# A Mamba block with a coupling layer on one core: ScalarE issues 29 of the transfers of each batch, x goes to another buffer, and two updates run by halves

## The chip, the cores and the metric

The program runs on one core of a Trainium2 chip. The metric is the device time of one execution in microseconds; the time of a kernel is the median of its runs. The engines are PE (TensorE), DVE (VectorE), ACT (ScalarE), POOL (GpSimd) and SP (SyncE, which computes nothing and only issues DMAs here). Every engine works through its own program in order; semaphores tie the programs together.

## The reference

Sixteen sequences of 1024 tokens with 256 channels go through two blocks, each with a residual and a layernorm.

```python
xi, res = split(x @ W_in.T + b_in)            # 512 channels each
xi = silu(causal depthwise conv(xi, 4 taps))
delta, B, C = split(xi @ W_x.T + b_x); delta = softplus(delta)   # 512, 16, 16
h = exp(delta * A) * h + delta * B * xi        # scan over tokens, 16 states per channel
y = (sum over states of h * C + xi * D) * silu(res)
x = layernorm(x + y @ W_out.T + b_out)
gf = global net of mean over tokens(x);  out = x
for _ in range(3):
    tf = sigmoid(small gelu net(out))          # one number per token
    out = out + (0.1 + range * 2 * (0.7 * gf + 0.3 * tf - 0.5)) * twist(out)
x = layernorm(x + out)
```

Twist swaps the two halves of the channels with signs. All is float32.

## The kernel before

**Units.** The scan of a batch is cut into 64 units: four blocks of 128 channels, each in four groups of 32 channels (a group on 128 partitions is 32 channels times 4 states), and four phases of 4 states for each group. There are 16 x 64 = 1024 units. For a unit ACT makes da = exp(delta_q * -A) in PSUM (L816), POOL makes dbx = u_q * b_quad in one of seven `work` buffers (L1060), DVE scans (L987), and the product with c_quad is made by DVE (L995) or, at the 26 positions of `POOL_AT`, by POOL three units later (L1067). PE sums the states into y_sum (L727), and every eight units DVE multiplies by the gates (L967).

**Side work.** All engines walk the same loop over t (one step per unit). At fixed positions within the period of 64 steps the tables `X_AT`, `RES_AT`, `DELTA_AT`, `O_AT` and so on place other work:
- for batch nb, one period ahead: x @ W_in, conv, silu (`SILU_AT` = 8, 32, 45, 55), gates ("r" tasks, into s_std), B and C rows ("c", into soft), delta for the next block ("d" tasks, ACT L938 to L944 into soft, DVE L1020 into delta, POOL L1082 makes u = delta * xi at DELTA_AT + 6 of each block);
- for batch f, one period behind: "o" (x + y @ W_out, L634 to L636, normalised by ACT into x1, which lies in the buffer `big`), "t" (transposed into oT), three cycles of the coupling net ("f", GELUs into big, tanh, DVE's products L1010 into big, POOL's updates of oT, L1075 and L1076), "g" (global net) and "e" (residual + oT + product, L665 to L668, normalised into oT, then stored to out).

PE's side work of step t is usually taken by DVE or ACT some steps later (`X_TAKE`, `O_RS` and so on). Three PSUM banks serve all of it, and a task waits until the one before has been read.

**Queues.** All DMAs are issued by SP, in the order of its program; where SP waits on a semaphore, everything behind it in its program waits too. SP's steps for step t are, in order: s_quad load, stores of delta and u, loads of delta_q and u_q (three copies of each; a group is loaded from DRAM after its store has landed and its slot is free), store of y, loads of yg, the x1 stores, the residual load (into the buffer yg), the out stores, the x_res load (L515, into oT, so it waits for the out stores), the gate stores (L405, four DMAs for each quarter), the x_feat load (L367), the bc stores (L536), and the loads of b_quad and c_quad. b_quad of phase 3 is loaded at position 63, behind three loads of c_quad, and is needed at the fourth unit of the next batch (unit 67 counted from this period's start).

**Around x_res.** x_res holds the batch's x for the residual of "o" and is read by PE at L636, after the four matmuls on yg; PE waits for both yg and x_res before the first matmul of "o". `first_gates` of batch 0 lie in s_std, big and oT.

Of the kernel before, what the change touches and what calls it, by code (L numbers as in the profile page):

```python
# [5 lines left out]
ALU = mybir.AluOpType  # L6
# [3 lines left out]
P = 128  # L10
BATCH, SEQ, DM = 16, 1024, 256
DI, NS, TAPS = 512, 16, 4
L = 512
DC = DI // P
# [72 lines left out]
RESST_AT = (4, 28, 47, 61)  # L87
X1ST_AT = (15, 16)
RES_IN_AT = 28
XRES_AT = 66  # L90
OUT_AT = (64, 64)
XFEAT_AT = 48
BCST_AT = 54
# [123 lines left out]
def build(nc, x, xT, weights, vectors, out):  # L217
# [7 lines left out]
    with ExitStack() as ctx:  # L225
# [65 lines left out]
        x_res = oT[:, :, :].rearrange("p m t -> p (m t)").rearrange("p (k c) -> p k c", c=DM)  # L291
# [73 lines left out]
        def _(sp):  # L365
# [37 lines left out]
            def store_gates(nb, n, gates, signal):  # L403
                for c in range(QUAD):
                    sp.dma_start(res_dram[nb % 2, n, c].rearrange("k p t -> p k t"),  # L405
                                 gates[GROUP * c:GROUP * c + GROUP, :].rearrange("p (k t) -> p k t", k=QUAD)) \
                      .then_inc(signal, 16)
# [63 lines left out]
            for t in range(FIRST, END):  # L471
# [20 lines left out]
                for h in range(2):  # L492
                    if (f := batch_at(t - PERIOD, X1ST_AT[h])) is not None:
                        sp.wait_ge(o_norm, 4 * f + 2 * h + 2)
                        sp.dma_start(x1_dram[f, h * L:(h + 1) * L, :].rearrange("(k p) c -> p k c", p=P),
                                     x1[:, 4 * h:4 * h + 4, :]).then_inc(x1_stored[h], 16)
                if (f := batch_at(t - PERIOD, RES_IN_AT)) is not None:
                    for h in range(2):
                        sp.wait_ge(x1_stored[h], 16 * (f + 1))
                    sp.wait_ge(o_ready, 4 * f + 4)  # L500
                    sp.dma_start(residual, x1_dram[f].rearrange("(k p) c -> p k c", p=P)).then_inc(re_in, 16)
                for h in range(2):
                    if (f := batch_at(t - PERIOD, OUT_AT[h])) is not None:
                        sp.wait_ge(e_norm, 4 * f + 2 * h + 2)
                        for r in range(2):
                            sp.dma_start(out[f, h * L:(h + 1) * L, :].rearrange("(n r p) c -> r p n c", p=P, r=2)[r],
                                         oT[:, r, h * L:(h + 1) * L].rearrange("p (n c) -> p n c", n=2)) \
                              .then_inc(out_done[h], 16)
                if (f := batch_at(t, XRES_AT)) is not None:
                    if f == 0:  # L510
                        sp.wait_ge(first_stored[DC - 1], 64)
                    if f:
                        for h in range(2):
                            sp.wait_ge(out_done[h], 32 * f)
                    sp.dma_start(x_res, x[f].rearrange("(k p) c -> p k c", p=P)).then_inc(xr_in, 16)  # L515

                for n in range(DC):
                    if ahead == RESST_FIRST[n]:
                        sp.wait_ge(r_taken, 2 * n + 2)
                        store_gates(0, n, first_gates[n], first_stored[n])  # L520
                    if (nb := batch_at(ahead, RESST_AT[n])) is not None and nb:
                        sp.wait_ge(res_ready, DC * (nb - 1) + n + 1)
                        store_gates(nb, n, s_std, res_stored)
                nb = 0 if ahead == XFEAT_FIRST else batch_at(ahead, XFEAT_AT)
                if nb is not None and nb + 1 < BATCH and (nb or ahead == XFEAT_FIRST):
                    sp.wait_ge(r_ready, 8 * nb + 8)
                    load_x_feat(nb + 1)
                nb = 0 if ahead == BCST_FIRST else batch_at(ahead, BCST_AT)
                if nb is not None and (nb or ahead == BCST_FIRST):
                    for j in range(PHASE):  # L530
                        if nb:
                            sp.wait_ge(c_in_[j], 16 * nb)
                            sp.wait_ge(b_in_[j], 16 * nb)
                    sp.wait_ge(c_taken, nb + 1)
                    for k in range(QUAD):
                        sp.dma_start(bc_dram[:, QT * k:QT * k + QT], first_or(nb, first_rows, bc_rows)[GROUP * k:GROUP * k + GROUP, :]) \  # L536
                          .then_inc(bc_stored, 16)
# [20 lines left out]
        def _(pe):  # L558
# [65 lines left out]
            def couple(kind, f, n, bank):  # L624
                shared = banks[:, bank, :]
                if kind == "o":
                    pe.wait_ge(yg_in[n % 2], 64 * (2 * f + n // 2 + 1))
                    if n == 0:
                        pe.wait_ge(xr_in, 16 * (f + 1))
                    for r in range(2):  # L630
                        tb = 2 * n + r
                        half = shared[:, r * DM:(r + 1) * DM]
                        for k in range(4):
                            pe.matmul(half, yg[:, n % 2, k, r * P:r * P + P], w_out[:, k, :], start=k == 0, stop=False)  # L634
                        pe.matmul(half, eye, b_out, start=False, stop=False)
                        mm = pe.matmul(half, eye, x_res[:, tb, :], start=False, stop=True)  # L636
# [503 lines left out]
```

## Time and profile before

| | us |
|---|---|
| median of 3 runs | 4038.7 |
| lowest, highest | 4038.14, 4043.2 |
| the profiled execution | 4040.28 |
| its span, first to last instruction | 4038.5 |
| mean granted TensorE clock | 0.946 of full speed |

| engine | busy us | share |
|---|---|---|
| POOL | 3644.6 | 90% |
| PE | 3524.4 | 87% |
| DVE | 3429.6 | 85% |
| ACT | 2959.0 | 73% |

The span has a start of 60 us (weights, the first conv), sixteen periods of some 240 us, and an end of about 140 us in which the last batch's coupling runs alone. An idle time in brackets stands before the instruction of its row, with what ended it.

### The profile page before, as it was taken

How to read it: one execution, taken by the hardware profiler on the slowest of the kernel's cores; microseconds unless marked ns; L12 is line 12 of the kernel's file. 1: busy time of each engine (PE TensorE's matmuls, PEld its weight loads, DVE VectorE, ACT ScalarE, POOL GpSimd, SP SyncE). 2: the span in 40 equal slices, each digit the busy share in tenths (PEclk: the TensorE clock that was granted, in tenths of full speed). 3: DMA queues.
4: the chain of work that ended last, by engine and by line, in shares of the span. 5: the costliest groups of instructions: out<-in, count | busy, mean ns of one | idle time of the engine just before them, and what ended most of it. 6: DMA issues, size and time to landing. Idle time of an engine off the chain costs nothing. (4 is left out here: it accounts for less than half of the span.)

```text
span 4038.5 us, 51729 instructions
## 1 busy us (share of the span) xinstructions
PE 3524.4 (87%) x18776; PEld 1611.5 (40%) x18776; DVE 3429.6 (85%) x2508; ACT 2959.0 (73%) x3918; POOL 3644.6 (90%) x1604
## 2 busy tenths in 40 slices
PE   7669989899998998989898998989989898897766
PEld 3224353443434344353443434344353443434233
DVE  4988988889898898989889898898989889898861
ACT  4447868778786877868777786877868777785753
POOL 4999999999999999999999999999999999999860
PEclk9779999999999999999999999999999999998888
DMA  5354373543536354373644546454363544546320
GB/s 182 130 175 154 128 230 120 188 152 130 186 130 224 129 191 138 122 229 120 197 148 155 159 152 200 140 187 129 133 218 123 194 149 158 160 138 199 127 86 31
DMA packets 329645, 630.04 MB, mean 156 GB/s; under 512 B 27952, under 2 KB 226608, under 8 KB 329136
## 3 DMA queue, kind: packets, MB, share of 16 engines
q1 hardware_dynamic: 329392, 626.74, 47.0%
q8 instruction: 150, 2.46, 0.3%
q14 instruction: 103, 0.84, 0.1%
HBM read 456.76 MB, written 169.87 MB: 155 GB/s over the span
## 5 line engine op out<-in xcount | busy, mean ns | idle before, releaser
L1060 POOL TENSOR_TENSOR work<-u_q,b_quad 128x1024 f32<-128x1024 f32 x1024 | 2397.3, 2372 | 138.2 <-DMA u_q<-u_scratch 97.1
L816 ACT ACTIVATE da<-delta_q,neg_a 128x1024 f32<-128x1024 f32 x1024 | 1126.3, 1112 | 600.9 <-DVE work L995 430.8
L987 DVE TENSOR_TENSOR_SCAN da<-da,work 128x1024 f32<-128x1024 f32 x608 | 1389.9, 2286 | 151.4 <-ACT da L816 119.7
L1067 POOL TENSOR_TENSOR work<-work,c_quad 128x1024 f32<-128x1024 f32 x416 | 985.2, 2368 | 11.6 <-DVE work L987 11.3
L987 DVE TENSOR_TENSOR_SCAN work<-da,work 128x1024 f32<-128x1024 f32 x416 | 945.9, 2278 | 29.9 <-ACT da L816 28.1
L727 PE MATMUL y_sum<-work,v_all 128*32 128x256 f32 x8192 | 613.3, 399 | 303.3 <-POOL work L1067 190.7
L995 DVE TENSOR_TENSOR work<-da,c_quad 128x1024 f32<-128x1024 f32 x608 | 743.9, 1224 | 28.6 <-DMA c_quad<-bc_scratch 4.6
L752 ACT ACT_TABLE_LOAD x563 | 722.3, 1283 | 14.5 <-DMA v_all<-in_vectors 3.9
L727 PEld LDWEIGHTS y_sum<-work,v_all 128*32 128x32 f32 x8192 | 199.8, 110 | 771.0 <-issue 259.3
L613 PE MATMUL banks<-xi,w_all 128*128 128x512 f32 x1024 | 479.8, 612 | 9.4 <-ACT g_act L797 5.1
L600 PE MATMUL banks<-xi,taps 128*128 128x512 f32 x984 | 453.2, 606 | 0.0
L681 PE MATMUL banks<-oT,w_all 128*128 128x512 f32 x768 | 389.7, 635 | 16.8 <-POOL oT L1076 16.7
L606 PE MATMUL banks<-x_feat,w_all 128*128 128x512 f32 x512 | 278.6, 684 | 27.5 <-DVE big L1010 26.7
L613 PEld LDWEIGHTS banks<-xi,w_all 128*128 128x128 f32 x1024 | 188.2, 192 | 259.4 <-issue 237.4
L634 PE MATMUL banks<-w_all,yg 128*128 128x256 f32 x1024 | 262.6, 402 | 30.8 <-DMA oT<-in_x 30.8
L591 PE MATMUL banks<-x_feat,w_all 128*128 128x512 f32 x512 | 256.0, 636 | 26.5 <-ACT big L787 17.2
L600 PEld LDWEIGHTS banks<-xi,taps 128*128 128x128 f32 x984 | 179.4, 191 | 244.1 <-issue 244.1
L787 ACT ACTIVATE big<-banks,v_all 128x512 f32<-128x512 f32 x336 | 218.9, 685 | 66.8 <-PE banks L681 47.0
L1082 POOL TENSOR_TENSOR soft<-delta,xi 128x1024 f32<-128x1024 f32 x64 | 151.2, 2362 | 112.1 <-DVE delta L1020 112.1
L634 PEld LDWEIGHTS banks<-w_all,yg 128*128 128x128 f32 x1024 | 200.9, 200 | 85.6 <-issue 58.5
L681 PEld LDWEIGHTS banks<-oT,w_all 128*128 128x128 f32 x768 | 136.0, 196 | 197.5 <-issue 183.3
L1010 DVE TENSOR_TENSOR big<-banks,oT 128x1024 f32<-128x1024 f32 x96 | 112.6, 1214 | 93.5 <-PE banks L703 93.5
(86 smaller groups left out, 3270.3 us busy)
## 6 DMA issues: line engine op xcount, KB each, us to landing
delta_q<-delta_scratch SPq DMA_DIRECT2D x256, 512.0 KB, 5.8
u_q<-u_scratch SPq DMA_DIRECT2D x256, 512.0 KB, 6.1
delta_scratch<-delta SPq DMA_DIRECT2D x64, 512.0 KB, 2.9
u_scratch<-soft SPq DMA_DIRECT2D x64, 512.0 KB, 2.9
b_quad<-bc_scratch SPq DMA_DIRECT2D x64, 512.0 KB, 4.7
c_quad<-bc_scratch SPq DMA_DIRECT2D x64, 512.0 KB, 7.1
s_quad<-res_scratch SPq DMA_DIRECT2D x128, 256.0 KB, 4.1
y_scratch<-s_quad SPq DMA_DIRECT2D x128, 256.0 KB, 3.2
```

What stands on the lines that cost most here:

```text
L600: mm = pe.matmul(banks[:, bank, to:], taps[:, m, k, :], xi[:, nb % 2, m, half * L + to - s:half * L + L - s], start=k == 3, stop=k == 0)
L606: mm = pe.matmul(banks[:, bank, :], w_in[:, k, DI + m * P:DI + m * P + P], x_feat[:, k, half * L:half * L + L], start=k == 0, stop=k == 1)
L613: mm = pe.matmul(banks[:, bank, :], w_x[:, k, m * P:m * P + P], xi[:, nb % 2, k, half * L:half * L + L], start=k == 0, stop=k == 3)
L634: pe.matmul(half, yg[:, n % 2, k, r * P:r * P + P], w_out[:, k, :], start=k == 0, stop=False)
L681: mm = pe.matmul(shared, w1[:, k, m * P:m * P + P], oT[:, k, half * L:half * L + L], start=k == 0, stop=k == 1)
L727: mm = pe.matmul(y_sum[GROUP * i:GROUP * i + GROUP, cols], fold, work[:, un % WORK, QT * i:QT * i + QT], start=False, stop=done)
L752: nc.scalar.preload_act_table_set(name)
L816: act.activation(da[:, t % 2, :], delta_q[:, slot, :], ACT.Exp, scale=neg_a[:, t % PERIOD:t % PERIOD + 1]).then_inc(da_ready, 1)
L987: dve.tensor_tensor_scan(dst, da[:, t % 2, :], work[:, slot, :], 0.0, ALU.mult, ALU.add) \
L995: dve.tensor_tensor(work[:, slot, :], da[:, t % 2, :], c_quad[:, j, :], ALU.mult).then_inc(prod_dve, 1)
L1060: pool.tensor_tensor(work[:, slot, :], u_q[:, copied, :], b_quad[:, j, :], ALU.mult) \
L1067: pool.tensor_tensor(work[:, un % WORK, :], work[:, un % WORK, :], c_quad[:, un % PHASE, :], ALU.mult) \
```

## The change

ACT issues the DMAs of what it makes: the x1 stores, the out stores, the gate stores of batches 1 and later, their bc stores, and also the x_feat load (from batch 2 on), the residual load and the x_res load. They stand in ACT's program some steps after the instruction that makes the data, with the same waits; the first batch's gate and bc stores stay with SP. x_res lies in `big` (the x1 buffer) and not in oT; it is loaded at position 63 instead of 66 and waits for the batch before's "e" products on PE (`e_ready`) instead of the out stores. The wait for the out stores moves to ACT's first "t" take. In "o" PE multiplies x_res and b_out first and waits for yg only then; in "e" it waits for the last coupling product only after three matmuls. POOL's two updates are made half by half, and PE's first matmuls of the next cycle wait for their own half.

```diff
-XRES_AT = 66
+XRES_AT = 63
-        x_res = oT[:, :, :].rearrange("p m t -> p (m t)").rearrange("p (k c) -> p k c", c=DM)
+        x_res = x1
@@ PE, "o"
-                    pe.wait_ge(yg_in[n % 2], 64 * (2 * f + n // 2 + 1))
                     if n == 0:
                         pe.wait_ge(xr_in, 16 * (f + 1))
                     for r in range(2):
...
+                        pe.matmul(half, eye, x_res[:, tb, :], start=True, stop=False)
+                        pe.matmul(half, eye, b_out, start=False, stop=False)
+                        if r == 0:
+                            pe.wait_ge(yg_in[n % 2], 64 * (2 * f + n // 2 + 1))
                         for k in range(4):
-                            pe.matmul(half, yg[:, n % 2, k, r * P:r * P + P], w_out[:, k, :], start=k == 0, stop=False)
-                        pe.matmul(half, eye, b_out, start=False, stop=False)
-                        mm = pe.matmul(half, eye, x_res[:, tb, :], start=False, stop=True)
+                            mm = pe.matmul(half, yg[:, n % 2, k, r * P:r * P + P], w_out[:, k, :],
+                                           start=False, stop=k == 3)
@@ PE, first matmuls of a cycle
-                            pe.wait_ge(updated, (CYCLES - 1) * f + c)
+                            pe.wait_ge(updated, 2 * ((CYCLES - 1) * f + c - 1) + half + 1)
@@ ACT, in its loop over t
+                    for h in range(2):
+                        if pos == O_AT[2 * h + 1] + O_RS + 1:
+                            act.wait_ge(o_norm, 4 * f + 2 * h + 2)
+                            act.dma_start(x1_dram[...], x1[:, 4 * h:4 * h + 4, :]).then_inc(x1_stored[h], 16)
+                        if pos == E_AT[2 * h + 1] + O_RS + 1:
+                            act.wait_ge(e_norm, 4 * f + 2 * h + 2)
+                            for r in range(2):
+                                act.dma_start(out[...], oT[...]).then_inc(out_done[h], 16)
+                    if pos == RES_IN_AT:
...
+                        act.dma_start(residual, x1_dram[f].rearrange("(k p) c -> p k c", p=P)).then_inc(re_in, 16)
...
+                if (f := batch_at(t, XRES_AT)) is not None:
+                    if f == 0:
+                        act.wait_ge(first_stored[1], 64)
+                        act.wait_ge(first_stored[2], 64)
+                    else:
+                        act.wait_ge(e_ready, 4 * f)
+                    act.dma_start(x_res, x[f].rearrange("(k p) c -> p k c", p=P)).then_inc(xr_in, 16)
...
+                        if pos == SILU_AT[m] + 1:
+                            act.wait_ge(res_ready, DC * (nb - 1) + m + 1)
+                            for c in range(QUAD):
+                                act.dma_start(res_dram[...], s_std[...]).then_inc(res_stored, 16)
+                    if pos == RES_AT[7] + RES_TAKE + 1 and nb + 1 < BATCH:
+                        act.wait_ge(r_ready, 8 * nb + 8)
+                        act.dma_start(x_feat[:, :, :], xT[nb + 1].rearrange("(k p) t -> p k t", p=P)).then_inc(xf_in, 16)
+                    if pos == BC_AT + BC_TAKE + 1:
...
+                        for k in range(QUAD):
+                            act.dma_start(bc_dram[:, QT * k:QT * k + QT], bc_rows[...]).then_inc(bc_stored, 16)
@@ POOL
-                            pool.wait_ge(f_prod, 2 * cycle + 2)
-                            pool.tensor_tensor(oT[:, 0, :], oT[:, 0, :], big[:, 1, :], ALU.add)
-                            pool.tensor_tensor(oT[:, 1, :], oT[:, 1, :], big[:, 0, :], ALU.subtract).then_inc(updated, 1)
+                            for half in range(2):
+                                cols = slice(half * L, half * L + L)
+                                pool.wait_ge(f_prod, 2 * cycle + half + 1)
+                                pool.tensor_tensor(oT[:, 0, cols], oT[:, 0, cols], big[:, 1, cols], ALU.add)
+                                pool.tensor_tensor(oT[:, 1, cols], oT[:, 1, cols], big[:, 0, cols], ALU.subtract) \
+                                    .then_inc(updated, 1)
```

## Rows read from the trace of the kernel before

**Rows 1.** The page, busy time, share of the span and instructions of each engine

```profile
PE 3524.4 (87%) x18776; PEld 1611.5 (40%) x18776; DVE 3429.6 (85%) x2508; ACT 2959.0 (73%) x3918; POOL 3644.6 (90%) x1604
```

**Rows 2.** Waits of POOL, 60 to 3900 us: us in total, times, longest

```profile
POOL work L1060 <- DMA u_q<-u_scratch: 97.1, 44, 4.0
POOL soft L1082 <- DVE delta L1020: 77.9, 20, 7.0
POOL work L1060 <- DMA b_quad<-bc_scratch: 37.0, 17, 10.4
```

**Rows 3.** Waits of SP's queue, whole span

```profile
SPq L405 <- ACT s_std L918: 366.1, 31, 16.2
...
SPq L367 <- PE banks L606: 145.7, 15, 10.3
```

**Rows 4.** Waits of all engines, whole span: DVE's scan

```profile
DVE da L987 <- ACT da L816: 119.7, 135, 16.1
...
DVE da L987 <- POOL work L1060: 29.9, 35, 3.0
```

**Rows 5.** Timeline of POOL, one period: start, duration, row, idle before

```profile
1864.68 2.36 POOL L1060 TENSOR_TENSOR work<-u_q,b_quad 128x1024 f32<-128x1024 f32 x1 [0.51 <-DMA u_q<-u_scratch]
...
1920.94 2.35 POOL L1067 TENSOR_TENSOR work<-work,c_quad 128x1024 f32<-128x1024 f32 x1 [0.46 <-DVE work L987]
...
1935.36 7.01 POOL L1060 TENSOR_TENSOR work<-u_q,b_quad 128x1024 f32<-128x1024 f32 x3 [2.77 <-DMA u_q<-u_scratch]
...
1956.22 2.39 POOL L1082 TENSOR_TENSOR soft<-delta,xi 128x1024 f32<-128x1024 f32 x1
...
1969.57 2.34 POOL L1060 TENSOR_TENSOR work<-u_q,b_quad 128x1024 f32<-128x1024 f32 x1 [1.72 <-DMA u_q<-u_scratch]
...
1980.50 4.67 POOL L1060 TENSOR_TENSOR work<-u_q,b_quad 128x1024 f32<-128x1024 f32 x2 [1.64 <-DMA b_quad<-bc_scratch]
```

**Rows 6.** Timeline of SP's queue, the same period

```profile
1857.18 1.79 SPq L405 DMA_DIRECT2D res_scratch<-s_std  x4
...
1928.27 0.39 SPq L367 DMA_DIRECT2D x_feat<-in_xT  x1
...
1929.27 0.53 SPq L400 DMA_DIRECT2D u_q<-u_scratch  x1
```

**Rows 7.** Timeline of PE, the same period

```profile
1944.74 0.64 PE L727 MATMUL y_sum<-work,v_all 128*32 128x256 f32 x8 [1.39 <-POOL work L1067]
...
1971.41 0.39 PE L668 MATMUL banks<-v_all,big 128*128 128x128 f32 x2
```

**Rows 8.** Timeline of DVE, the same period

```profile
1907.73 2.30 DVE L987 TENSOR_TENSOR_SCAN da<-da,work 128x1024 f32<-128x1024 f32 x1 [1.50 <-ACT da L816]
...
1955.39 0.75 DVE L1020 SCALAR_TENSOR_TENSOR delta<-banks,v_all,soft 128x512 f32<-128x512 f32 x1 [0.30 <-ACT soft L944]
```

**Rows 9.** Timeline of ACT: the exp of unit 64 of this period

```profile
1968.25 1.12 ACT L816 ACTIVATE da<-delta_q,neg_a 128x1024 f32<-128x1024 f32 x1 [3.19 <-DMA delta_q<-delta_scratch]
```

**Rows 10.** Busy time in 1972 to 1976 us; last: clock, DMA share, GB/s

```profile
1972.00:1976.00 4.00, 1.86 (x32) 0.64 (x24) 3.69 (x3) 1.12 (x1) 4.00 (x2) 1.00 0.92 353
```

**Rows 11.** Groups of instructions: busy us, mean ns of one, idle before

```profile
L1010 DVE TENSOR_TENSOR big<-banks,oT 128x1024 f32<-128x1024 f32 x96 | 112.6, 1214 | 93.5 <-PE banks L703 93.5
...
L1075 POOL TENSOR_TENSOR oT<-oT,big 128x1024 f32<-128x1024 f32 x32 | 75.2, 2351 | 90.6 <-DVE big L1010 90.6
...
L1037 POOL TENSOR_TENSOR coef<-v_all 128x1 f32<-128x1 f32 x1 | 0.2, 193 | 0.1
```

**Rows 12.** Timeline of PE, the end of the run

```profile
3920.20 3.75 PE L634 MATMUL banks<-w_all,yg 128*128 128x256 f32 x8 [14.76 <-DMA oT<-in_x]
...
3975.46 9.67 PE L681 MATMUL banks<-oT,w_all 128*128 128x512 f32 x16 [7.00 <-POOL oT L1076]
...
4020.82 0.67 PE L665 MATMUL banks<-yg,v_all 128*128 128x256 f32 x2 [1.28 <-DVE big L1010]
```

**Rows 13.** Timeline of SP's queue, the end of the run

```profile
3910.39 1.94 SPq L441 DMA_DIRECT2D yg<-y_scratch  x4
```

**Rows 14.** The page, DMA issues: count, KB each, median us to landing

```profile
yg<-y_scratch SPq DMA_DIRECT2D x256, 128.0 KB, 3.7
```

More of the change, by code:

```diff
@@ L401, in load_u, with store_first_gates @@
                              .broadcast_to([GROUP, QUAD, SEQ])).then_inc(uq_in[slot], 16)
[L403 removed]
+            def store_first_gates(n):
                 for c in range(QUAD):
[L405 to L407 removed]
+                    sp.dma_start(res_dram[0, n, c].rearrange("k p t -> p k t"),
+                                 first_gates[n][GROUP * c:GROUP * c + GROUP, :].rearrange("p (k t) -> p k t", k=QUAD)) \
+                      .then_inc(first_stored[n], 16)
             def load_s_quad(pair):
@@ L491, in _ @@
                         load_yg(f, n)
[L492 to L515, printed above, removed]
                 for n in range(DC):
@@ L519, in _ @@
                         sp.wait_ge(r_taken, 2 * n + 2)
[L520 to L534, printed above, removed]
+                        store_first_gates(n)
+                if ahead == XFEAT_FIRST and BATCH > 1:
+                    sp.wait_ge(r_ready, 8)
+                    load_x_feat(1)
+                if ahead == BCST_FIRST:
+                    sp.wait_ge(c_taken, 1)
                     for k in range(QUAD):
-                        sp.dma_start(bc_dram[:, QT * k:QT * k + QT], first_or(nb, first_rows, bc_rows)[GROUP * k:GROUP * k + GROUP, :]) \
+                        sp.dma_start(bc_dram[:, QT * k:QT * k + QT], first_rows[GROUP * k:GROUP * k + GROUP, :]) \
                           .then_inc(bc_stored, 16)
@@ L659, in couple @@
                     pe.wait_ge(re_in, 16 * (f + 1))
-                    pe.wait_ge(f_prod, 2 * (CYCLES * f + CYCLES - 1) + n // 2 + 1)
                     for r in range(2):
@@ L667, in couple @@
                             pe.matmul(half[:, m * P:m * P + P], oT[:, m, tokens], eye, start=False, stop=False)
+                        if r == 0:
+                            pe.wait_ge(f_prod, 2 * (CYCLES * f + CYCLES - 1) + n // 2 + 1)
+                        for m in range(2):
                             mm = pe.matmul(half[:, m * P:m * P + P], big[:, 1 - m, tokens], minus if m else eye,
@@ L819, in _ @@
                 for f, pos in couplings(t):
+                    for h in range(2):
+                        if pos == O_AT[2 * h + 1] + O_RS + 1:
+                            act.wait_ge(o_norm, 4 * f + 2 * h + 2)
+                            act.dma_start(x1_dram[f, h * L:(h + 1) * L, :].rearrange("(k p) c -> p k c", p=P),
+                                          x1[:, 4 * h:4 * h + 4, :]).then_inc(x1_stored[h], 16)
+                        if pos == E_AT[2 * h + 1] + O_RS + 1:
+                            act.wait_ge(e_norm, 4 * f + 2 * h + 2)
+                            for r in range(2):
+                                act.dma_start(out[f, h * L:(h + 1) * L, :].rearrange("(n r p) c -> r p n c", p=P, r=2)[r],
+                                              oT[:, r, h * L:(h + 1) * L].rearrange("p (n c) -> p n c", n=2)) \
+                                   .then_inc(out_done[h], 16)
+                    if pos == RES_IN_AT:
+                        for h in range(2):
+                            act.wait_ge(x1_stored[h], 16 * (f + 1))
+                        act.wait_ge(o_ready, 4 * f + 4)
+                        act.dma_start(residual, x1_dram[f].rearrange("(k p) c -> p k c", p=P)).then_inc(re_in, 16)
                     for n in range(4):
@@ L826, in _ @@
                             act.wait_ge(t_ready, 4 * f + n + 1)
+                            if n == 0 and f:
+                                for h in range(2):
+                                    act.wait_ge(out_done[h], 32 * f)
                             act.activation(oT[:, m, half * L:half * L + L], banks[:, BANK_OF["t", f, n], :],
```

16 lines of the change are left out of this document (11 added, 5 removed).

## Prediction

> **What bounds the kernel now.** I read the busy shares first, then who POOL waits for, then SP's own waits, then one period of 240 us (one batch, 64 units) engine by engine, then the end of the run. POOL is busy 90%, DVE 85%, PE 87%, ACT 73% [rows 1]. That makes POOL look like the bound, with idle time in three groups: 97 us until u_q lands, 78 us until delta is made, 37 us until b_quad lands [rows 2]. The u_q waits are SP's doing: SP is an in-order queue that stood 366 us before the gate stores and 146 us before the x_feat loads, with u_q loads queued behind [rows 3]. In the period that I read, the u_q stall of 2.77 us before unit 56 [rows 5] comes from a load issued at 1929.27, just behind the x_feat load at 1928.27 [rows 6], and the one at unit 36 from loads behind the four gate stores at 1857.18 [rows 6].
>
> The question is whether those stalls are on the path. Over the run DVE's scans waited 119.7 us for ACT's da and only 29.9 us for POOL's products [rows 4]. So POOL is not ahead of a chain that hangs on it: in the second half of a period ACT and DVE set the pace. Three rows say so. DVE's scan at 1907.73 waits 1.50 us for ACT [rows 8]; POOL at 1920.94 waits 0.46 us for DVE [rows 5]; and POOL's u at 1956.22 starts 0.08 us after delta's second half is done (1955.39 + 0.75) [rows 5, 8]. POOL's lost time in this half is mostly slack that it must give back at the next of these meetings.
>
> **Part 1: loads no longer stand behind SP's waits.** The unit-36 stall (0.51 us here; the 44 u_q waits of the run average 2.2 us [rows 2]) ends before POOL next meets DVE (a product with a wait of 0.46 at 1920.94), so I count 0 for it; if all of it were on the path, 2 us per batch. The unit-56 stall of 2.77 us is different. It delays POOL's product of unit 55, for which PE waited 1.39 us just before the next block's delta matmuls [rows 7], and those lead to ACT's soft, DVE's delta and POOL's u. Without the stall the next thing late is PE's own work, after ACT's silu. So the worth is 1.39 of the 2.77 us: -1.39 us x 14 batches = -19 us. Bounds: 0 and -2.8 x 14 = -39 us.
>
> **Part 2: 29 DMA issues per batch move to ACT.** 16 gate stores, 4 bc stores, 4 out stores, 2 x1 stores, residual, x_res and x_feat. Four gate stores took SP 1.79 us [rows 6], 0.45 each; the trace of before has no DMA issued by ACT, so this is the nearest row. Total 29 x 0.45 = 13 us per batch, on an engine with 27% idle. Most falls where ACT is waiting anyway, so it costs nothing there. Where ACT runs dense and DVE waits for its da, it counts: the gate stores after silu at positions 33 and 46 (the scan that waited 1.50 us for ACT at 1907.73 is at 46, [rows 8]). Each burst is queued behind an exp of 1.1 us (1.12 in [rows 9]). If the queue issues while that exp runs, 1.8 - 1.1 = 0.7 us is left; otherwise 1.8; and 0 if ACT issues faster than SP. I take 0.6 each, 1.2 per batch, against the 1.39 won in part 1 on the same chain: net -0.2 us x 14 = -3 us. Bounds: -1.39 and +2.2 us per batch (-19 to +31 us). The waits ahead of these DMAs are on ACT's own results or on transfers long done, with one exception.
>
> **Part 3: x_res.** ACT now waits at position 63 for all four "e" products. PE finishes the fourth at 1971.8 [rows 7]. ACT's next exp (unit 64) started at 1968.25 [rows 9] and would start at about 1972.2, 4 us late; what is queued behind is that exp, the third normalise and the first two out stores. DVE's scan of unit 64 slips about 0.6 us, which the b_quad stall three units later swallows. I count 0; bound +0.6 x 15 = +9 us.
>
> But the load itself moves. It used to go out after the out stores; now 1 MB of x, and 0.5 MB of out, start at about 1972, when the DMA engines already moved 353 GB/s at a busy share of 0.92 [rows 10] and the last b_quad load is still to come. POOL waited 1.64 us for that b_quad at 1980.50 [rows 5], in the part of the period in which POOL does set the pace. 1.5 MB at 353 GB/s is 4.2 us if all of it went ahead; the gate stores of 0.5 MB that stood there move away, worth 1.5 us; and two queues share instead of queueing. Between -0.5 and +3 us per batch; I take +0.8: +0.8 x 15 = +12 us. The Trainium skill (DMA: Bandwidth & Descriptors, Queues, rings and completion order) says that an SDMA engine goes round the queue rows packet by packet. By it SP's b_quad is slowed by x_res and not put behind it; no row of before shows two issuing queues.
>
> The longest u_q stall is 4.0 us [rows 2], not 2.77; for the few at unit 56 that are longer than in my period I count another -3 us in all.
>
> **Part 4: updates by halves.** POOL runs 64 ops of 2.35 us [rows 11] as 128. With 193 ns for a one-column op [rows 11], half an op is 0.193 + 511 x 2.11 ns = 1.27 us, so a pair costs 0.2 us more: 0.8 us per batch. It falls where POOL waits for DVE at the next meeting (0.46 us at 1920.94) and has just been freed of the unit-36 stall: 0. Without this cover, +12 us.
>
> **Part 5: the end of the run.** After the last scan nothing hides. PE waited 14.76 us for x_res until 3920.20 [rows 12]; now only yg is waited for. Its four issues began at 3910.39 and took 1.94 us [rows 13], landing takes 3.7 us [rows 14]: 3916.0, and up to 1 us less, because the out stores no longer stand ahead. With two of the matmuls done before, PE has saved about 5.5 us. Each of the two updates: PE waited 7.00 us until 3975.46 [rows 12]. Behind the first half of DVE's product there used to be the second half (1.21 us) and two whole updates (4.70 us) [rows 11]; now it is one pair of halves, 2.54 us: 1.21 + 4.70 - 2.54 = 3.4 us earlier, twice, 6.7 us. The second half is ready before PE asks. "e" starts three matmuls before the product: 0.9 of the 1.28 us of wait at 4020.82 [rows 12]. Together -13 us, bounds -9 and -17.
>
> **Sum.** -13 - 3 - 3 + 12 = -7, plus about -1 for x_res's own wait gone within periods: -8 us. The profiled execution took 4040.3 us (span 4038.5), 1.6 above the median of 4038.7: 4032 by the profile, 4030.5 by the median. Predicted: 4030.
>
> **Rivals.**
> 1. Slower, x_res in front of b_quad. Place: POOL at unit 67. For: DMA near saturation there [rows 10]; each us lost is POOL's and DVE's together. Against: the queues share, and the gate stores leave. At 3 us per batch: 4038.7 - 13 - 6 + 45 = 4065. It makes the kernel slower from about 1.4 us per batch (21 us against 13 + 6). Chance 0.17.
> 2. ACT becomes the bound: issues aren't hidden under the exp, 1.8 us per burst: 4038.7 - 13 + 31 = 4057 with contention at 0. For: ACT is dense and DVE waits for it [rows 4]. Against: 27% idle overall. Chance 0.12.
> 3. The SP stalls are worth more: ACT's issues are hidden and contention is nil: 4038.7 - 13 - 19 - 5 = 4002. If POOL's time counts in full (2 + 2.8 us per batch), 4038.7 - 13 - 70 = 3956. For: POOL's 90%. Against: POOL has to meet DVE between. Chance 0.24 for near 4002, 0.05 for near 3956.
> 4. The issuer does not matter: only the order and the end change, 4038.7 - 13 = 4026. The Trainium skill (DMA: Bandwidth & Descriptors, Issuing engines are not separate DMA queues) says that issuing from several engines saves only the time that the sequencer takes to issue. By it parts 1 and 2 are nearly nothing; but the rows show that SP's queue loses its time in waits, 366 us at one line [rows 3], which the rule does not speak of. Chance 0.07.
>
> The forecast itself (4012 to 4045) has 0.35. A measurement of this kernel can tell about 0.2%, 8 us. Below 4030.6: rivals 3 and 4 and not quite half of the forecast, 0.50; within 8 us either way 0.24; above 4046.8 rivals 1 and 2 less a little, 0.26. The range for 8 in 10 reaches from inside rival 3 to inside rival 1: 3985 to 4068.
>
> **What would show it.** Right: SP's waits at the gate stores and x_feat gone, POOL's u_q idle down from 97 us to about 40 (the wait at unit 64 stays), but POOL's waits for delta and for DVE's products up by nearly as much. ACT's DMA issues visible at about 0.45 us. POOL's b_quad waits up from 37 us to about 50. In the tail PE starts "o" near 3915 instead of 3920 and the two 7 us waits become 3.7. Wrong: a period well below 239 us, with POOL's waits for DVE not grown, means that the SP stalls were on the path; b_quad waits of 70 us or more mean rival 1; DVE's wait for da far above 120 us means rival 2.

## The result and the profile after

| | before | after |
|---|---|---|
| median us (8 runs each) | 4038.09 | 4060.28 |
| lowest, highest | 4033.76, 4046.72 | 4051.1, 4067.87 |
| ratio of the times, 95% interval | | 1.0046 [1.0035, 1.0058] |
| span of the profiled execution | 4038.5 | 4058.3 |

The change makes the kernel 0.46% slower, about 20 us. The forecast was 4030 us, 8 us faster than before. Of the executions that the later sections compare, two (5821 us and 4160 us, at a granted clock of 0.55 and 0.87) ran in a slower state of the chip and are left out.

The first thing to read is where along the run the 20 us lie. The table is worked out from the starts of DVE's 1024 scans, as means over the periods 1 to 14, in us.

| stretch | before | after | difference |
|---|---|---|---|
| units 0 to 8 of a period | 27.0 | 28.8 | +1.8 |
| 8 to 15 | 30.0 | 30.8 | +0.8 |
| 15 to 28 | 51.9 | 51.5 | -0.4 |
| 28 to 36 | 28.1 | 27.5 | -0.6 |
| 36 to 46 | 38.8 | 38.7 | -0.1 |
| 46 to 56 | 36.0 | 36.0 | 0 |
| 56 to 64 | 29.5 | 29.6 | +0.1 |
| period, from scan 64 to scan 960, by 14 | 241.23 | 242.86 | +1.63 |
| first period; last period | 227.3; 233.0 | 228.4; 235.8 | +1.1; +2.8 |
| last scan to the end | 135.1 | 128.6 | -6.5 |

14 x 1.63 = 22.8, with 1.1 and 2.8 that is 26.7, less 6.5 is 20.2; the first scan comes 0.5 earlier. The loss is in units 0 to 15 of each period, right behind the place where x_res is loaded (position 63 of the period before); the units behind them win back 1.0 us.

The waits of POOL from 60 us on, beside [rows 2] (us in total, times, longest):

```profile
POOL soft L1096 <- DVE delta L1031: 76.7, 33, 7.0
POOL work L1071 <- DMA b_quad<-bc_scratch: 76.6, 17, 11.4
POOL work L1071 <- DMA u_q<-u_scratch: 46.4, 27, 3.8
POOL work L1078 <- DVE work L998: 42.6, 60, 3.5
```

The u_q waits are halved (97.1 to 46.4), and POOL now waits for DVE's products instead (L1078, 42.6 us; before it was 11.3 us). So 31 of the 51 us are slack which changed its name. The b_quad waits doubled, 37.0 to 76.6 us, and one of the 17 is the one at the start of the run. DVE shows whose time that is. Its scan's waits from 300 to 3900 us, first before, then after:

```profile
DVE da L987 <- ACT da L816: 99.9, 132, 3.3
DVE da L987 <- POOL work L1060: 20.4, 28, 1.4
```

```profile
DVE da L998 <- ACT da L781: 110.1, 145, 3.6
DVE da L998 <- POOL work L1071: 38.1, 27, 2.6
```

The wait for POOL's products grew from 20.4 to 38.1 us, since POOL's stalls reach DVE; the wait for ACT grew by 10 only.

SP's waits changed their name too. Its 366.1 us at the gate stores [rows 3] are gone, but an in-order queue then stands at the next thing that isn't ready, here the store of y. That wait, before and after, over the whole span:

```profile
SPq L428 <- DVE s_quad L967: 500.5, 54, 23.4
```

```profile
SPq L423 <- DVE s_quad L978: 848.6, 69, 23.4
```

One such stall, read engine by engine. ACT's queue (ACTq is ACT's DMA issue) around position 63, in the trace of after:

```profile
1990.31 0.40 ACTq L862 DMA_DIRECT2D big<-in_x  x1
1990.81 1.12 ACT L781 ACTIVATE da<-delta_q,neg_a 128x1024 f32<-128x1024 f32 x1 [7.56 <-PE banks L633]
1990.83 1.23 ACTq L793 DMA_DIRECT2D out<-oT  x2
```

SP's queue and POOL at the same time:

```profile
1986.41 6.89 SPq L441 DMA_DIRECT2D c_quad<-bc_scratch  x3
1993.39 0.69 SPq L441 DMA_DIRECT2D b_quad<-bc_scratch  x1
...
1992.67 4.69 POOL L1071 TENSOR_TENSOR work<-u_q,b_quad 128x1024 f32<-128x1024 f32 x2
2001.79 4.66 POOL L1071 TENSOR_TENSOR work<-u_q,b_quad 128x1024 f32<-128x1024 f32 x2 [4.43 <-DMA b_quad<-bc_scratch]
```

The 1 MB of x_res leave at 1990.31, 0.5 MB of out at 1990.83, and the last b_quad load at 1993.39. POOL can go on at 2001.79, 8.4 us after the issue; before it was 1974.91 to 1980.50, 5.6 us. (The medians over batches 2 to 15 are 8.6 and 5.5 us.) The stall is 4.43 us where it was 1.64 [rows 5]. What the DMA engines moved behind the issue (the last numbers of a row: clock, DMA share, GB/s), before and after:

```profile
1974.00:1978.00 4.00, 2.41 (x33) 0.87 (x34) 3.65 (x6) 0.78 (x2) 4.00 (x3) 1.00 0.80 323
1978.00:1981.00 3.00, 3.00 (x8) 1.32 (x9) 3.00 (x4) 2.90 (x9) 1.36 (x2) 1.00 0.56 224
```

```profile
1994.00:1998.00 4.00, 2.62 (x20) 1.01 (x21) 3.97 (x8) 3.24 (x8) 3.36 (x2) 1.00 1.01 336
1998.00:2002.00 4.00, 4.00 (x11) 1.85 (x10) 3.90 (x3) 3.48 (x6) 0.21 (x1) 1.00 1.03 409
```

Before, the engines had room while b_quad was on its way (a share of 0.80, then 0.56). After, they are full until it has landed.

### The profile page after: what moved, and what is told of

Same layout as the page of the kernel before. It is cut to its first block and busy times, and to the rows that moved or that the text cites. A ratio compares the mean times of both kernels' runs of the same rounds, so it can differ in the third digit from the quotient of the medians.

```text
span 4058.3 us, 51746 instructions
## 1 busy us (share of the span) xinstructions
PE 3531.5 (87%) x18776; PEld 1621.1 (40%) x18776; DVE 3429.1 (84%) x2508; ACT 2960.5 (73%) x3918; POOL 3655.3 (90%) x1668
## 5 line engine op out<-in xcount | busy, mean ns | idle before, releaser
L1071 POOL TENSOR_TENSOR work<-u_q,b_quad 128x1024 f32<-128x1024 f32 x1024 | 2394.9, 2367 | 127.3 <-DMA b_quad<-bc_scratch 76.6
L1078 POOL TENSOR_TENSOR work<-work,c_quad 128x1024 f32<-128x1024 f32 x416 | 983.0, 2363 | 42.6 <-DVE work L998 42.6
L574 PE MATMUL banks<-xi,w_all 128*128 128x512 f32 x1024 | 493.1, 626 | 9.5 <-ACT g_act L762 5.1
L598 PE MATMUL banks<-w_all,yg 128*128 128x256 f32 x1024 | 245.3, 383 | 4.5 <-DMA yg<-y_scratch 4.5
```

Source lines behind the costliest of these rows:

```text
L574: mm = pe.matmul(banks[:, bank, :], w_x[:, k, m * P:m * P + P], xi[:, nb % 2, k, half * L:half * L + L], start=k == 0, stop=k == 3)
L598: mm = pe.matmul(half, yg[:, n % 2, k, r * P:r * P + P], w_out[:, k, :], start=False, stop=k == 3)
L1071: pool.tensor_tensor(work[:, slot, :], u_q[:, copied, :], b_quad[:, j, :], ALU.mult) \
L1078: pool.tensor_tensor(work[:, un % WORK, :], work[:, un % WORK, :], c_quad[:, un % PHASE, :], ALU.mult) \
```

## The experiments

All ratios are to the kernel before, run beside the changed one each time, with a 95% interval; its median lay between 4038 and 4046 us, so ratios are to be compared and not times. "Period" and "tail" (last scan to the end) are those of the table above. The theory at the outset: rival 1's mechanism, x_res and out in front of b_quad. Its rivals: a wait that ACT took over, and the cost of ACT's issues.

**x_res for one batch only.** It leaves out 15 of the 16 x_res loads; the wait for the "e" products stays.

```diff
+                    if f == 0:
                         act.dma_start(x_res, x[f].rearrange("(k p) c -> p k c", p=P)).then_inc(xr_in, 16)
@@ PE, "o"
-                        pe.wait_ge(xr_in, 16 * (f + 1))
+                        pe.wait_ge(xr_in, 16)
```

> The changed kernel, but x is loaded into the x1 buffer for batch 0 only; the 15 later loads of 1 MB are left out (later batches add a stale buffer), while ACT still waits for the e products at the same place. My theory (x_res competes with the last b_quad load, +2 us per batch, and with the last store of y in the tail): POOL's b_quad waits fall from 76.6 us to 40 or less, the b_quad load lands in about 5.6 us after its issue and not 8.3, and the time falls by 25 to 35 us, to about 0.994 to 0.998 of the kernel before. Rival (ACT standing up to 8.6 us before e_ready delays the exp of unit 64 and with it everything): time stays within 5 us of the changed kernel, 1.004 to 1.006, whatever the b_quad wait does. Second rival (the out stores are what collides): b_quad waits stay above 60 us.

Measured: 0.9925 [0.9904, 0.9946]. The b_quad waits are 36.2 us, the period 240.07, units 0 to 8 take 26.3 us. The wait on ACT is still there and harmless:

```profile
ACT da L781 <- PE banks L633: 100.5, 14, 8.1
```

So it is the load's bytes, and not the wait that stands ahead of it. (The next run, which has no such wait though it has the bytes, has a period only 0.3 us shorter.) The gain over the changed kernel, 1.2% or 49 us, is more than the 25 to 35 us that I expected.

**x_res by SP, behind the last b_quad and c_quad loads.** All is kept, and only the place differs.

```diff
-    (ACT) act.wait_ge(e_ready, 4 * f) ; act.dma_start(x_res, ...)
+    (SP, after load_b and load_c of the step) sp.wait_ge(e_ready, 4 * f) ; sp.dma_start(x_res, ...)
```

> The changed kernel, but SP issues the x_res load, in its own order behind the last loads of b_quad and c_quad (same wait for the e products). Theory of contention: b_quad goes first in one queue, b_quad waits fall to about 45 us (the out stores still share), ACT's wait for e_ready is gone; time 15 to 25 us below the changed kernel, 0.998 to 1.001 of before. If only the ACT wait mattered: the same gain here but none in the run without the loads. If neither: 1.0046 as the changed kernel.

Measured: 0.9901 [0.9883, 0.9919], 4007.27 us: faster than before by 1%, and well below the 0.998 to 1.001 that I expected. The period is 239.74, 3.1 us less than after, and units 0 to 8 take 26.5 us. SP's queue and POOL:

```profile
1967.37 0.65 SPq L441 DMA_DIRECT2D b_quad<-bc_scratch  x1
1968.11 0.55 SPq L441 DMA_DIRECT2D c_quad<-bc_scratch  x1
1968.71 0.58 SPq L514 DMA_DIRECT2D big<-in_x  x1
...
1972.23 4.67 POOL L1071 TENSOR_TENSOR work<-u_q,b_quad 128x1024 f32<-128x1024 f32 x2 [0.91 <-DMA b_quad<-bc_scratch]
```

With x_res issued 1.3 us behind it instead of 3.1 us ahead of it, b_quad is there 4.9 us after its issue instead of 8.4; the median is 5.5 us, as before the change. One more thing moves in this run: ACT no longer stands at the "e" wait, so the first out half goes out 6.7 us ahead of b_quad instead of 2.8.

**Is it the issuer or the place?** Two runs cross the two: x_res stays on ACT but goes out three units later, and x_res goes to SP but ahead of the last b_quad load.

```diff
-XRES_AT = 63
+XRES_AT = 66
```

> The changed kernel with the x_res load still issued by ACT but at position 66 instead of 63, so some 4 to 6 us after the last b_quad load is issued. Theory (what collides is the time at which 1 MB starts, not ACT as issuer): b_quad waits 45 to 60 us (the first out half still collides), ACT's wait for e_ready is gone, time 15 to 35 us below the changed kernel, 0.996 to 1.001 of before; PE may wait a little for x_res before o. Rival (it has to be SP's queue, in order behind b_quad): within 8 us of the changed kernel.

```diff
+    (SP, ahead of load_b and load_c of the step) sp.wait_ge(e_ready, 4 * f) ; sp.dma_start(x_res, ...)
```

> The run with x_res by SP, but in SP's order the x_res load stands just ahead of the last b_quad load and not behind the last c_quad. One queue, 1 MB in front: at 353 GB/s that is 2.8 us more until b_quad lands. Theory (bandwidth ahead of b_quad is the whole harm): b_quad waits 34 + 15 x 2 to 3 = 65 to 80 us, the time about that of the changed kernel less its out part, 1.000 to 1.005 of before. Rival (two queues sharing is worse than one in order): b_quad waits under 50 us and a ratio under 0.995.

Measured: 0.9938 [0.9922, 0.9955] on ACT at 66, with b_quad waits of 42.9 us; and 1.0047 [1.0029, 1.0065] by SP ahead of b_quad, with 80.1 us, the same as after. One queue, SP's, in the run that is slow:

```profile
1986.39 0.86 SPq L505 DMA_DIRECT2D big<-in_x  x1
1987.34 0.54 SPq L441 DMA_DIRECT2D b_quad<-bc_scratch  x1
...
1995.31 4.66 POOL L1071 TENSOR_TENSOR work<-u_q,b_quad 128x1024 f32<-128x1024 f32 x2 [4.92 <-DMA b_quad<-bc_scratch]
```

From b_quad's issue to POOL's start are 8.0 us, against 8.4 with two queues (medians 7.8 and 8.6; in this run b_quad also goes out 0.7 us later for POOL, since SP first waits for "e" and issues x_res). The issuer is not the cause of the loss; the megabyte started ahead of b_quad is. Between ACT at 66 and SP behind the quads 0.4% remain. By the profiled executions (spans 4016.8 and 4005.4 us) nearly all of it lies in the periods, 0.76 us each; the tail is only 1.0 us longer, though the late x_res makes PE wait 10.6 us for it there. Why ACT at 66 is the worse place was not tested.

**The out stores.** Both halves at position 67, x_res still on ACT at 63.

```diff
-                        if pos == E_AT[2 * h + 1] + O_RS + 1:
+                        if pos == E_AT[3] + O_RS + 1:
```

> The changed kernel; both halves of the out stores are issued by ACT at position 67, behind the last normalise, instead of the first half at position 64. x_res stays on ACT at 63. Theory (x_res's 1 MB does most of the harm, the first 0.5 MB of out a part): b_quad waits fall from 76.6 to 55 to 70 us, time 3 to 12 us below the changed kernel (1.002 to 1.004 of before). Rival (the out stores collide, x_res not): b_quad waits near 37 us and 0.993 of before.

Measured: 0.9988 [0.9976, 0.9999]; b_quad waits 54.3 us, period 241.58. The first out half, a third of the bytes ahead of b_quad, is worth 0.58%, or 23 us, where I expected 3 to 12: 1.3 us of each period, and 4 us at the end of the run (most of these at another granted clock, see Part 5 below).

The runs together show what b_quad's way costs. The table is worked out from the traces, medians over batches 2 to 15 in us; a start with a minus lies ahead of b_quad's issue, one with a plus behind it.

| run | x_res starts | first out half starts | b_quad's issue to POOL's start |
|---|---|---|---|
| before | +11.5, SP | +1.9, SP | 5.5 |
| after | -3.4, ACT | -2.8, ACT | 8.6 |
| x_res for one batch only | not loaded | -3.0, ACT | 5.5 |
| out late | -3.1, ACT | +5.7, ACT | 6.7 |
| x_res by SP ahead of b_quad | -0.7, SP | -7.3, ACT | 7.8 |
| x_res by SP behind | +1.3, SP | -6.7, ACT | 5.5 |
| x_res by ACT at 66 | +4.6, ACT | -6.7, ACT | 6.0 |
| x_res and bc by SP, out late (below) | +1.3, SP | +5.5, ACT | 5.0 |

Against the 5.0 us with nothing of the two ahead, half a megabyte of out alone costs 0.5 us, x_res alone on ACT 1.7, both together 3.6: what these transfers cost doesn't add up. x_res right ahead in b_quad's own queue costs 2.3 us (7.8 against 5.5).

**Part 1: what the two stalls on SP were worth.** One puts the x_feat load back on SP at its old place, the other the gate stores.

```diff
-    (ACT) act.wait_ge(r_ready, 8 * nb + 8) ; act.dma_start(x_feat, ...)
+    (SP, position 48) sp.wait_ge(r_ready, 8 * nb + 8) ; load_x_feat(nb + 1)
```

> The changed kernel, but SP issues the x_feat load at its old place. Theory: the u_q stall of 2.8 us before unit 56 comes back (u_q waits from 46 up to about 85 us). By the prediction it cost 1.39 us per batch on PE ahead of the delta matmuls; but the changed kernel gives that back in ACT's wait for bc_scratch, so I expect 0 to 8 us slower than the changed kernel (1.0046 to 1.0065 of before). Rival (not on the path at all): within 2 us. Rival (fully on the path): 20 to 39 us slower, 1.009 to 1.014.

```diff
-    (ACT, SILU_AT[m] + 1) act.wait_ge(res_ready, ...) ; four act.dma_start(res_dram, ...)
+    (SP, positions 4, 28, 47, 61) sp.wait_ge(res_ready, ...) ; four sp.dma_start(res_dram, ...)
```

> The changed kernel, but SP issues the gate stores again at its old positions. Theory: SP's waits there only made POOL stall where it has slack against DVE and ACT, so the u_q waits rise from 46 us by about 25 us (the stall at unit 36 comes back), POOL's waits for delta and for DVE's products fall by about as much, and the time stays within 5 us of the changed kernel; the scans from unit 36 to 46 and 46 to 56 stay at 38.6 and 36.0 us. Rival (the SP stalls at the gate stores were on the path): 15 us or more slower than the changed kernel. Rival (ACT pays for these issues): faster by 10 us or more.

Measured: x_feat on SP 1.0090 [1.0072, 1.0109], period 244.18 (my expectation was too low; this is my rival "fully on the path", at its lower edge); gates on SP 1.0035 [1.0024, 1.0046], period 242.85. POOL's waits, first with x_feat on SP, then with the gates on SP:

```profile
POOL work L1072 <- DMA u_q<-u_scratch: 82.0, 37, 4.4
POOL work L1079 <- DVE work L999: 20.8, 31, 3.4
```

```profile
POOL work L1071 <- DMA u_q<-u_scratch: 73.1, 41, 3.8
POOL work L1078 <- DVE work L998: 25.2, 25, 3.8
```

Both bring back u_q waits, 35.6 and 26.7 us. In the first the program loses 0.44%, 18 us (1.32 us per period, 0.8 of them in units 56 to 64, behind the stall that comes back); in the second it loses nothing. POOL's sums don't tell the two apart: its waits for DVE's products shrink by 21.8 us in the first and by 17.4 in the second. Where the stall stands does.

**Part 2: ACT's wait for the bc stores.** The ACT timeline of after shows a wait that my working had not:

```profile
1960.15 1.28 ACT L717 ACT_TABLE_LOAD   x1
1960.16 1.28 ACTq L870 DMA_DIRECT2D res_scratch<-s_std  x3
...
1964.98 1.12 ACT L781 ACTIVATE da<-delta_q,neg_a 128x1024 f32<-128x1024 f32 x1 [0.99 <-DVE work L998]
1965.30 1.74 ACTq L882 DMA_DIRECT2D bc_scratch<-soft  x4
1968.29 0.69 ACT L949 ACTIVATE soft<-banks,soft_bias 128x512 f32<-128x512 f32 x1 [2.19 <-DMA bc_scratch<-soft]
```

The bc stores now stand behind an exp that waits for DVE, so they go out late, and ACT's next write to soft waits until they have landed: 35.5 us in 15 waits, before 3.8 in 2. This kernel gives the bc stores back to SP at position 54.

> The changed kernel, but SP issues the bc stores of batches 1 and later again, at its old place. Theory: in the changed kernel the store is queued on ACT behind the exp of position 58, so ACT's next soft waits for its landing (35.5 us in 15 waits) and the 1.4 us won on PE before the delta matmuls are lost. With SP: that wait is gone or under 5 us, delta of the last block is made about 1 to 1.4 us earlier per batch, time 12 to 20 us below the changed kernel (1.000 to 1.002 of before). Rival: the delta chain isn't what the next batch waits for (it waits for u_q and b_quad transfers), then the time falls by less than 5 us though the wait is gone.

Measured: 1.0028 [1.0014, 1.0042]; ACT's wait falls from 35.5 to 17.3 us, the period by 0.3 us. Beside after's 1.0046 that is some 7 us, and the intervals overlap: a small loss, likely but not certain, and less than the 12 to 20 us that I expected. Half of ACT's wait is still there.

**Part 4 and 5: updates whole again.**

```diff
-                            for half in range(2): ... oT[:, 0, cols] ... oT[:, 1, cols] ... .then_inc(updated, 1)
+                            pool.wait_ge(f_prod, 2 * cycle + 2)
+                            pool.tensor_tensor(oT[:, 0, :], ...); pool.tensor_tensor(oT[:, 1, :], ...).then_inc(updated, 2)
```

> The changed kernel with POOL's two updates whole again (64 ops of 2.35 us instead of 128 of 1.27), PE's next cycle still waiting for both. Theory: inside the periods the halves cost and bring nothing; in the tail they save 3.3 us twice. So this run is 5 to 8 us slower than the changed kernel (1.0058 to 1.0066 of before), and PE's two waits of 3.8 us in the tail are 7 us again. Rival (128 ops cost POOL, the busiest engine, 0.8 us per batch on the path): this run is 5 us or more faster than the changed kernel.

Measured: 1.0060 [1.0043, 1.0076]. The period is 242.79 (after 242.86), so the halves cost nothing within it; the tail is 133.7 us, 5.1 more than after. PE's two waits in the tail are 14.2 us with whole updates; in after they are:

```profile
3997.86 9.64 PE L646 MATMUL banks<-oT,w_all 128*128 128x512 f32 x16 [3.75 <-POOL oT L1089]
...
4020.71 10.15 PE L646 MATMUL banks<-oT,w_all 128*128 128x512 f32 x16 [3.84 <-POOL oT L1089]
```

**SP issues everything.** Does the issuer matter at all? Every transfer is on SP at its old place, x_res late as in the second run, with the new order in "o" and "e" and the halves.

> The changed kernel with every DMA issued by SP, at the old places in SP's order, except x_res, which SP issues behind the last loads of b_quad and c_quad (into the x1 buffer, as in the run with x_res by SP). What is left of the change: the other buffer and place for x_res, the order of the matmuls in o and e, the updates by halves. Theory (the issuer is worth nothing in the periods, the ACT and DVE chain sets the pace from unit 28 on; the gain of the run with x_res by SP came from x_res and the end of the run): 0.990 to 0.995 of before, within 0.2% of the run with x_res by SP. Rival (freeing SP's queue is what makes that run fast, once the x_res collision is gone): 0.996 to 1.001, near before less the 6 to 10 us of the tail.

Measured: 0.9950 [0.9935, 0.9965], period 240.62, tail 121.6; u_q waits are back at 91.0 us, and SP stands again where it stood:

```profile
SPq L512 <- ACT s_std L930: 361.6, 31, 16.0
```

Against 0.9901 with ACT issuing, ACT's issuing is worth about 0.5%, 20 us, where my theory said less than 0.2%. That is about what the x_feat place was worth by itself (18 us above); no run splits it here. The other half of the gain over before needs no second queue.

**The mended versions.** First x_res and bc by SP and both out halves late; then also the last b_quad load a unit earlier, ahead of the second c_quad load.

> The run with x_res by SP (ratio 0.9901), with the bc stores on SP and the out stores of both halves at position 67 as well. Theory (each removes a cause found: bc landing before soft, sharing with b_quad): b_quad waits near 34 us or below, ACT's wait for bc landing under 20 us, ratio 0.985 to 0.990. Rival (the last block's delta isn't what the next batch waits for): within 0.1% of 0.990.

```diff
-LB_AT, LC_AT = (59, 55, 57, 63), (61, 62, 61, 63)
+LB_AT, LC_AT = (59, 55, 57, 62), (61, 63, 61, 63)
```

> Starts from the mended version (x_res, the bc stores and x_res behind the quads on SP, both out halves late) and changes only the order of two loads: the last b_quad load of a batch goes out at unit 62, ahead of the second c_quad load, instead of behind it. In the mended version POOL still waits 29.5 us in all for b_quad: one wait of 10.9 us at the start of the program and about 1.2 us per batch. Theory: that per-batch wait is the last thing that holds POOL, and through POOL the DVE, in the stretch around units 4 to 8. Then the b_quad waits fall to about 12 us in all, the period falls by 1.0 to 1.6 us, and the time against the kernel before is 0.984 to 0.988 of it. Rival: the wait is taken over by the next one, either c_quad (now later) or a DVE result that POOL needs; then the b_quad waits fall but another POOL or DVE wait grows by as much, and the time stays at 0.989 to 0.992.

Measured: 0.9904 [0.9887, 0.9921], no better than x_res alone moved, as the rival said: b_quad waits 29.5 us and ACT's wait for bc 17.5 us are as my theory had them, the time is not. So with x_res out of the way, neither the late out stores nor the bc stores on SP are worth more than the 10 us or so that the intervals leave. Then 0.9869 [0.9852, 0.9885], 3994.76 us, the fastest of all. In the last one POOL waits for b_quad only at the start of the run. POOL's two lines, first without, then with the earlier load:

```profile
POOL work L1078 <- DVE work L998: 46.1, 59, 3.4
...
POOL work L1071 <- DMA b_quad<-bc_scratch: 29.5, 17, 10.9
```

```profile
POOL work L1078 <- DVE work L998: 52.4, 63, 3.4
...
POOL work L1071 <- DMA b_quad<-bc_scratch: 11.9, 2, 10.5
```

Of the 17.6 us some went to waits for DVE (+6.3) and for u_q (+4.6). Units 8 to 15 take 1.1 us less, and units 15 to 46 take 0.8 us more. The times put it in the theory's range. The two profiled executions don't: both spans are 3995.8 us, and the periods are 239.27 and 239.03. They were the fastest execution of the one kernel and the slowest of the other, and the two intervals all but touch. That the order of these two loads is worth something is likely; how much, between 0 and 14 us, stays open.

## Why the prediction was wrong, step by step

The measured 4060 us lie within the stated 3985 to 4068, but the kernel became slower where the forecast was faster. Of the signs named in advance, "b_quad waits of 70 us or more mean rival 1" came: 76.6 us.

- **What bounds the kernel, and the unit-36 stall at 0: right.** The gates on SP bring 27 us of u_q waits back and cost nothing.
- **Part 1, -19 us for x_feat: right.** 18 us measured (the two intervals leave 6 to 30), 1.32 us per period against 1.39 in the working. The closeness of the two is in part luck: 0.5 of the 1.32 us lie outside units 56 to 64.
- **Part 2, issues on ACT at 1.2 us per batch (+17 us within the net of -3): wrong, it is 0.** An issue takes about what was expected (1.28 us for three, 1.74 for four, though 1.23 for the two of out), but the three at 1960.16 run beside ACT's table load. "Each burst is queued behind an exp" asked the right question, and of its three answers 0 was the right one. The bursts stand at positions 33 and 46 and the x_feat load at 51; the stretches 28 to 36, 36 to 46 and 46 to 56 take 27.5, 38.7 and 36.0 us, before 28.1, 38.8 and 36.0. Rival 2 falls with it.
- **Part 2, "the waits ahead of these DMAs are on ACT's own results or on transfers long done": true, and beside the point.** What delays a DMA on a computing engine is also the instruction before it, here an exp that waited for DVE. I had asked what queues behind the DMA's wait, but not what the DMA queues behind and who waits until it has landed. Some 7 us by one run, within the noise by another.
- **Part 3, x_res at +0.8 us per batch (+12 us): this term lost the case.** By the run with x_res moved behind b_quad it is 3.1 us per period, some 45 us, and 53 us (4058.3 less 4005.4) with the first and last periods and the end; some 3 of the 4.6 us at the end are a lower granted clock (Part 5). Rival 1 had the mechanism, its price (3 us per batch) and its total (4065, measured 4060), with a chance of 0.17. That its total fits is in part luck: it took 13 us for the end where 6.5 came, and 6 us for parts 1 and 2 where more came. Where the working went wrong: "1.5 MB at 353 GB/s is 4.2 us if all of it went ahead" was the right bound. I then took away 1.5 us for gate stores that leave, and discounted for two queues that share. But the way of b_quad grew by 3.1 us per batch all the same, so sharing and the gate stores together gave back about a quarter of 4.2 us, not four fifths. The Trainium skill (DMA: Bandwidth & Descriptors, Queues, rings and completion order) says that an SDMA engine goes round the queue rows packet by packet, which I had read as protection. Here b_quad took 7.8 us with 1 MB ahead in its own queue and 8.6 us with 1.5 MB ahead in the other, so the second queue did not save it; with 1 MB alone in the other queue it took 6.7 us. How much of that is the second queue and how much the earlier start (3.1 us ahead, against 0.7) can't be told from these runs.
- **Part 3, the "e" wait on ACT: nearly harmless, as said** (some 0.3 us per period between the first two runs), though it is 7.6 us each (106.9 us in 14 waits), not 4.
- **Part 4: right.** Half an op takes 1.27 us, and it costs nothing:

```profile
L1088 POOL TENSOR_TENSOR oT<-oT,big 128x512 f32<-128x512 f32 x64 | 81.2, 1269 | 83.3 <-DVE big L1021 83.3
```

- **Part 5, -13 us: half of it came, 6.5 us.** The two update waits went from 7.00 and 7.09 to 3.75 and 3.84 us, 6.5 us, as worked out. The start of "o" gained too: the first matmuls on yg start 13.3 us after the last scan's end, before 16.8, so 3.5 of the 5.5 us came. What took them back is a term that the working didn't have: PE's work from the first cycle's start to its first update wait took 22.3 us instead of 19.3, at a mean granted clock of 0.81 instead of 0.96 (with bc on SP 20.4 us at 0.92, with all on SP 18.8 us at 1.00: time times clock is 18.0 to 18.8 us in all four), and what follows the second update took 0.7 us more instead of less. PE in the tail of after:

```profile
3936.42 1.19 PE L593 MATMUL banks<-big,v_all 128*128 128x256 f32 x2 [4.73 <-DMA big<-in_x]
3937.40 1.06 PE L594 MATMUL banks<-v_all 128*128 128x256 f32 x2
3942.99 3.78 PE L598 MATMUL banks<-w_all,yg 128*128 128x256 f32 x8 [4.53 <-DMA yg<-y_scratch]
```

The last y store goes out at 3932.47 and SP issues yg at 3938.39, 5.9 us later, since that store lands beside x_res (issued 3929.86) and out (3930.28): it takes 5.9 us to land, before 2.2, and without x_res (first experiment) 2.4. It is the same competition as in the periods, a second time, and it holds back the 2 us that "o" lacks. PE waits 4.73 us for x_res as well, which the working had as long landed. With x_res behind the quads and all on SP the tail is 121.6 us, 13.5 less than before. That this comes to the forecast's number is in part luck: "o" starts 4.6 us earlier, the update waits are 6.5 us shorter, and the first cycle's work is 0.6 us shorter at the higher clock.

**The sum redone:** -18 (x_feat) - 6.5 (tail) + 7 (bc) + 3.1 x 14 to 15.5 batches, 43 to 48 (x_res and what it delays), is +26 to +31; measured +20. Without the uncertain 7 us for bc it is +19 to +24. Units 15 to 36 take 1.0 us less than before, and the shorter u_q stalls don't explain it: with the gates on SP it is 1.0 us as well (u_q waits 73.1 us), and with all on SP 0.7 us (91.0 us). The cause of that stays open.

And without x_res in the way the ratio is 0.9901, 3998 us on the forecast's base, where rival 3 had 4002. So the mechanisms of rival 1 and of rival 3 were both at work, and the forecast between them was right on neither; the working treated as alternatives what adds up.

## What to carry to other kernels

Before a transfer is moved, list the transfers that an engine is about to wait for within one landing time behind its new start: a megabyte started ahead of such a load cost it 2.3 us in its own queue, 1.7 us from another queue with 3 us of lead, and 3.6 us there together with half a megabyte more, which by itself cost 0.5. Where SP's queue stands in a wait, find which queued load reaches the path; one place (x_feat, 36 us of POOL's waits) was worth 18 us and another (the gates, 27 us) nothing. And where DMA engines are full for a few us, order the loads by when they are needed.

## What the runs showed of the hardware

- No cost of ACT's DMA issues to its compute is seen: three of them took 1.28 us beside a table load of 1.28 us, and the stretches 36 to 46 and 46 to 56 take 38.75 and 36.0 us with ACT issuing and x_res behind, 38.83 and 36.0 us with SP issuing everything.
- A 512 KB load was there for POOL 5.5 us after its issue with 1 MB started 1.3 us behind it, after 8.6 us with 1.5 MB started ahead of it in another queue, after 6.7 us with 1 MB ahead of it in another queue, and after 7.8 us with 1 MB ahead of it in its own queue (medians of the table above).
- In the tail PE's granted clock differed with the timing around it. The 25 us of the first coupling cycle, after and before:

```profile
3969.00:3994.00 25.00, 21.30 (x56) 9.24 (x56) 0.08 (x1) 10.71 (x23) 0.00 (x0) 0.77 0.12 37
```

```profile
3943.00:3968.00 25.00, 19.09 (x69) 9.03 (x67) 1.01 (x4) 12.63 (x29) 0.00 (x0) 0.98 0.20 63
```

0.77 of full speed against 0.98. PE had stood 4.73 and 4.53 us some 30 us before the window of after, but 14.76 us before that of before, and 2.58 us near its start in both, so idle time alone doesn't explain it. In after the clock was at its lower level (half) for 6.9 us in a row just there, in before it was not. The runs with x_res ahead don't all show it: with bc on SP the mean over the same work was 0.92. The cause stays open; what it cost is the 3.0 us of Part 5.
